# Joining the value products of a group's first and second tick into one burst

## What is computed

```python
x = x + 0.5 * ffn(layernorm(x))      # sigmoid(xr @ W_r.T) * (relu(xk @ W_k.T)**2 @ W_v.T), xr, xk mix x with the row before
q, k, v = split(layernorm(x) @ W_qkv + b_qkv)      # 16 heads, rotary positions on q and k
att = softmax(where(causal, q @ k.T / 4, -1e9))
x = x + (att @ v) @ W_proj + b_proj
x = x + 0.5 * ffn(layernorm(x))
```

## Time and profile before

| | |
|---|---|
| median of the runs | 3116.66 us (the lowest 3114.29) |
| profiled execution | 3112.07 us, span 3110.3 us |
| PE busy | 2962.3 us, 95% of the span |
| DVE busy | 2475.0 us, 80% |
| ACT busy | 2159.2 us, 69% |
| POOL busy | 1566.6 us, 50% |

### The profile page before, as it was taken

The page is one execution under the profiler, slowest core; times in us unless marked ns, Lnnn a source line. Parts: engine busy times, 40 slices in busy tenths (PEclk is TensorE's granted clock), DMA queues, the critical chain, the costliest instruction groups (busy, mean ns, idle before and its releaser), DMA issues.

```text
span 3110.3 us, 56224 instructions
## 1 busy us (share of the span) xinstructions
PE 2962.3 (95%) x18245; PEld 1665.9 (54%) x18245; DVE 2475.0 (80%) x7302; ACT 2159.2 (69%) x4802; POOL 1566.6 (50%) x2190
## 2 busy tenths in 40 slices
PE   6899999999999999999999999999999999999997
PEld 4444555555555555555555555555555555555444
DVE  3888888888888888888888887888888888887872
ACT  4477777777777777777777777777767777777664
POOL 5455555555455455555555455454555555454323
PEclk9899999999999999999999999999999999999999
DMA  3443343343434352342443333343442532433421
GB/s 99 79 84 65 64 100 66 83 90 72 86 77 88 69 97 67 76 99 60 91 87 68 88 77 84 80 85 76 79 93 59 98 81 67 93 76 71 83 60 39
DMA packets 202585, 245.49 MB, mean 79 GB/s; under 512 B 68405, under 2 KB 104245, under 8 KB 202293
## 3 DMA queue, kind: packets, MB, share of 16 engines
q1 hardware_dynamic: 202293, 241.90, 37.5%
HBM read 53.48 MB, written 51.38 MB: 34 GB/s over the span
## 4 chain that ended last, share of the span: by engine, by line
PE 66%; DVE 12%; ACT 8%; POOL 6%; issue 6%; DMA 1%; SPq 1%; POOLq 0%; DVEq 0%; ACTq 0%
PE ps_y L735 14%; PE ps_s L704 12%; PE ps_m L714 11%; PE ps_d L794 7%; PE ps_d L788 6%; PE ps_d L791 5%; PE ps_d L800 5%; ACT pt_sb L830 4%; DVE ps_m L943 3%; PE ps_d L781 3%; PE ps_d L742 2%; DVE mx_sb L946 2%; PE ps_d L804 2%; POOL pt_sb L1075 2%; DVE dif_sb L974 2%
## 5 line engine op out<-in xcount | busy, mean ns | idle before, releaser
L830 ACT ACTIVATE pt_sb<-ps_s 128x512 f32<-128x512 f32 (+1 forms) x3039 | 1451.6, 495 | 816.9 <-PE ps_s L704 806.7
L943 DVE CUSTOM_DVE_ANT_0 ps_m<-ps_m,mask_sb 128x128 f32<-128x128 f32 (+3 forms) x2048 | 990.3, 498 | 370.7 <-PE ps_m L714 355.9
L704 PE MATMUL ps_s<-qr_sb,kr_sb 99*128 99x512 bf16 (+1 forms) x3039 | 994.5, 329 | 50.4 <-ACT pt_sb L830 39.3
L714 PE MATMUL ps_m<-kr_sb,qr_sb 96*128 96x512 bf16 (+3 forms) x3072 | 1000.1, 329 | 37.9 <-DVE mx_sb L943 27.7
L946 DVE TENSOR_REDUCE mx_sb<-ps_m 128x1 f32<-128x512 f32 x1024 | 697.9, 682 | 105.7 <-PE ps_m L714 97.3
L1075 POOL TENSOR_SCALAR_AFFINE_SELECT pt_sb<-pt_sb 128x512 f32<-128x512 f32 x512 | 331.4, 647 | 833.8 <-ACT pt_sb L830 833.3
L735 PE MATMUL ps_y<-pt_sb,v_sb 128*32 128x512 f32 (+3 forms) x6144 | 589.9, 494 | 3.6 <-POOL pt_sb L1075 2.7
L704 PEld LDWEIGHTS ps_s<-qr_sb,kr_sb 99*128 99x128 bf16 x3039 | 291.8, 96 | 510.0 <-issue 229.7
L714 PEld LDWEIGHTS ps_m<-kr_sb,qr_sb 96*128 96x128 bf16 x3072 | 302.0, 98 | 319.2 <-DVE mx_sb L943 71.1
L800 PE MATMUL ps_d<-axn_sb,wqk_sb 128*128 128x256 f32 x1024 | 305.3, 396 | 3.9 <-ACT axn_sb L872 3.9
L735 PEld LDWEIGHTS ps_y<-pt_sb,v_sb 128*32 128x32 f32 x6144 | 154.6, 109 | 285.9 <-issue 258.3
(11 more groups left out here) (96 smaller groups left out, 3465.5 us busy)
## 6 DMA issues: line engine op xcount, KB each, us to landing
kr_sb<-part_sb SPq DMA_DIRECT2D x378, 128.0 KB, 4.4
qr_sb<-part_sb SPq DMA_DIRECT2D x378, 128.0 KB, 4.7
y_way<-yt_sb SPq DMA_DIRECT2D x128, 256.0 KB, 2.7
sw_sb<-qb_sb SPq DMA_DIRECT2D x496, 64.0 KB, 2.0
x_sb<-x SPq DMA_DIRECT2D x64, 256.0 KB, 2.8
yn_sb<-y_way SPq DMA_DIRECT2D x64, 256.0 KB
den_sb<-r_way SPq DMA_DIRECT2D x64, 256.0 KB
out<-x_sb SPq DMA_DIRECT2D x64, 256.0 KB, 2.2
```

The source lines that it names most:

```text
L704: eng.matmul(score_bank(slot)[:, 0:width], kr_sb[0:KR + NP, n % RS, j, kb * P:(kb + 1) * P], qr_sb[0:KR + NP, n % RS, j, q0:q0 + width], s ...
L714: eng.matmul(ps_m[:, u % NM, 0:width], qr_sb[0:KR, n % RS, j, i * P:(i + 1) * P], kr_sb[0:KR, n % RS, j, piece * QC:piece * QC + width], s ...
L830: eng.activation(pt_sb[:, buffer, j, column:column + width], score_bank(slot)[:, 0:width], ACT.Exp, scale=SCALE).then_inc(exped, 1)
L943: eng.tensor_tensor_reduce(ps_m[:, u % NM, 0:width], ps_m[:, u % NM, 0:width], mask_sb[:, m0:m0 + width], 1.0, -3e38, ALU.add, ALU.max, be ...
```

## The change

Tick 0 is put into the burst of tick 1. The burst that stood in slot 7 goes; the one in slot 11 has 16 instructions in place of 8, first those of tick 0, then those of tick 1, and raises `pved` by two. The planner does not read `BURSTS`, so the order of everything else stays as it is, on every engine. It holds for all 64 groups.

```diff
-BURSTS = [(0,), (1,), (2, 3), (4, 5), (6, 7), (8, 9), (10, 11)]
+BURSTS = [(0, 1), (2, 3), (4, 5), (6, 7), (8, 9), (10, 11)]
```

## The result

| | before | after |
|---|---|---|
| median | 3114.29 us (3110.61 to 3116.66) | 3164.51 us (3162.86 to 3166.68) |
| profiled execution, span | 3110.3 us | 3161.3 us |
| ratio | | 1.0163, 95% interval 1.0148 to 1.0178 |

The joined burst makes the kernel 1.6% slower, some 50 us by the medians and 51.0 us from span to span. The forecast was 3157, with 3120 to 3174 as the range. Direction and mechanism came as forecast; the loss was put at 40 us and is 50.

A forecast was written before the change was run, and what follows sets the result against it. PE, 95% busy, was taken as the bound, held in places by DVE and ACT. 33.9 (39 groups) + 2.0 (three) + 3.8 (first groups) + 0 (others) = 39.7 us on 3116.66: 3156.4, say 3157; range 3120 to 3174.

The forecast's parts named there:

- The cost of the joined burst: Slot 11: the longer burst takes 1.65 us, priced from ticks 8 and 9, against 0.78 for tick 1: 0.87 more.
- The advance of 0 in the 39 groups: Slots 10 and 11: DVE's maxima hold PE, so PE gains no time by slot 11; 0.87 each, 33.9 us.
- DVE gapless, so the maximum comes at the same time: Slots 7 to 11: DVE works off earlier work without gaps, so PE, free 1.09 us earlier, meets the same maximum.
- The advance in the first groups: A batch's first group, slot 9: xt_sb from ACT limits PE's gain to 0.58 of 1.09; cost 0.29, 13 groups, 3.8 us.
- The nine other groups, the start and the end: Nine groups at the kernel's start and end, -0.22 to +0.87 each: 0 together, bounds -2.0 and +7.8.
- Nothing is paid back after slot 11: Slots 12 on: PE's later waits shift with PE, so none of the 0.87 us comes back; taken as 0.
- the 42 groups: Groups held by DVE in slots 10 and 11: 39 at 0.87 (33.9 us), three with 0.2 us slack at 0.67 (2.0).
- The likeliest case: Whole kernel: the forecast itself, 3143 to 3170 us, chance 0.52.
- the third rival: All groups: no advance, 55.7 us, plus tenths in slots 12 to 19 from starved DVE and ACT; 3172 to 3190, chance 0.18.
- 0.22 us for each extra burst: Each group: one change of PE's tiling mode in and out, 0.12 exit and 0.10 entry, saved if all 1.09 is usable.

The follow-up runs named there:

- the addition alone: Kernel before with tick 0's value products made a second time at the head of slot 11's burst, slot 7's burst kept: 3166.78 us, ratio 1.0167.
- The reliefs: Two-burst and joined kernels, DVE's maxima of slots 3-8 over 128 columns: 3115.15, 3135.7 us; also POOL's cosine product over an eighth: 3116.86, 3118.84.
- join_third: Kernel before with the joined burst in slot 8 in the third group of each batch alone (16 groups): 3112.73 us, ratio 1.0000.
- join_third_late: Kernel before with the joined burst in slot 8 only in the third groups of batch elements 2 to 13 (12 groups): 3111.82 us, ratio 0.9984.
- relief_split: Kernel before, two bursts kept, with DVE's maxima of the units in slots 3 to 8 taken over 128 columns only: 3115.15 us, ratio 1.0007.
- the removal alone: Kernel before with slot 7's burst left out in groups 1 to 63 and nothing added: 3115.03 us, ratio 0.9995.

## Why the prediction was right, and where it was off

**The cost of the joined burst** was put at 0.87 and is 0.86 in every kind of group (the addition alone). The pair of ticks 8 and 9 was a true price for it.

**The advance of 0 in the 39 groups.** Held: 0.86 us lost in the regular ones, 36.1 in all against 33.9, some 5 of it the clock's (below). The step "DVE gapless, so the maximum comes at the same time" was the right test; the two timelines above show it to 0.01 us. The reliefs show it as a cause for the third group, and for the fourth only both together. For the second it is read from the waits alone; in the kernel after, PE stands there for exps too, 0.25 us in slot 9 on average.

I had called DVE's stretch of work DVE's own. Its length was partly POOL's, in the kernel before already. DVE and POOL in the fourth group of the earlier trace rows:

```profile
1571.91 1.15 DVE L974 SCALAR_TENSOR_TENSOR dif_sb<-dif_sb,mur_sb,fxn_sb 128x256 f32<-128x256 f32 x1
1572.98 0.68 DVE L997 TENSOR_TENSOR sw_sb<-sw_sb,sin_sb 128x512 f32<-128x512 f32 x1
```

```profile
1571.34 1.44 POOL L1116 TENSOR_TENSOR qb_sb<-qb_sb,cos_sb 128x512 f32<-128x512 f32 x1
```

The product of L974, 0.48 us in the median, takes 1.15 and ends 0.28 us after the cosine product (1573.06 against 1572.78). The sine product comes behind both and takes its 0.68; only in the relieved kernels is it the one that is held. In the third group of the earlier trace rows the sine product of 1.14 us ends at 1524.87, 0.53 us after POOL's select of tick 0:

```profile
1523.70 0.64 POOL L1075 TENSOR_SCALAR_AFFINE_SELECT pt_sb<-pt_sb 128x512 f32<-128x512 f32 x1 [1.25 <-ACT pt_sb L830]
```

That did not change the forecast, since all this was under way before the burst: the same rows in the kernel after are 1.15 and 1.14 us long.

**The advance in the first groups** was mis-sized: 0.58 forecast, 0.40 measured (0.86 - 0.46), 13 x 0.17 = 2.2 us. I let PE start when its input was written. It starts 0.14 us later, and here the wait is new, so the delay counts. The last 0.04 us are not explained.

**The nine other groups, the start and the end** were put at 0, with +7.8 as the bound; they took 3.3 + 1.0 + 2.2 = 6.5 us. Most of it is group 0 with 5.2, and that is the clock, not the burst. Before, group 0 has PE busy for 65.47 of 78.60 us at a mean granted clock of 0.93; after, for 71.15 of 83.80 us at 0.86, with the same 348 instructions. The start differs by that much between kernels that are the same there: group 0 is 4.1 us longer than before in the profile of `join_third` (clock 0.88) and 0.5 shorter in that of `join_third_late` (0.93).

**Nothing is paid back after slot 11.** Held: slots 12 to 47 differ by 0.00 in the regular groups, and the addition alone costs 51.8 of 55.7. This was the step that I was least sure of.

**What was missing** in the sum, beside the 0.17 of the first groups, is the clock: three second groups (17, 29 and 53) took 2.4 to 2.6 us where the others took 0.86, some 5 us together. With 2.2 of the first groups, 6.5 of the edges and 2.6 in the 42 groups (36.1 + 2.4 against 33.9 + 2.0, these three counted), the sum of 39.7 becomes 51.0. Three second groups and group 0 make some 10 of the 11.3 us that the sum was short; other groups of the edges go both ways. So a part of the miss is what the clock happened to be in one profile. The likeliest case's own range, 3143 to 3170, held; the third rival, dearer by starved dense steps, did not come: DVE stood 1.24 us as it foresaw, but no later wait grew from it.

## What to carry to other kernels

An engine that is busy for 95% can still be held in a stretch of a few slots, and there its work costs no time, up to the end of what the other engine has in hand: look at the stretch between the place a piece of work leaves and the place it goes to, and ask if the engine that hands over there has gaps. If it has none, the leaving work gains nothing and the arriving work costs all. Work that seems to be cut up at a price (0.22 us for each extra burst) may be the cover that lets another engine catch up, so price its removal and its addition apart, by two small experiments. Taking away what holds the engine may only uncover the next one that is level with it, as ACT's exps in the second groups. And judge such a move group by group: one and the same edit gave -0.59 us in one kind of group and +1.35 in another.

## What the runs showed of the hardware

**DVE and POOL on SBUF.** DVE's sine product (float32, two inputs in SBUF), when it starts while POOL's cosine product is running, ends 0.55 us after it: 1.76 us with 1.21 of overlap, 0.80 with 0.26 when the cosine product is cut to an eighth, 0.69 alone. The tail is the same for both overlaps, so the sine product makes next to no progress meanwhile, and its length in a profile is not its own. The rows above show the same with POOL's select (0.53 us after it) and with the product of L974, half as wide (0.28). Who starts first matters: in `relief_split` at 191.38 the sine product starts 0.05 us ahead of the cosine product and takes its 0.69, and the cosine product takes 1.77 where it took 1.44. The Trainium skill (SBUF — State Buffer, Who interferes with whom) has the shared ports as an exclusive lock, also for a DVE instruction with both inputs in SBUF against a POOL instruction that reads it; the trace agrees.

**The clock, with short waits before it.** In the kernel after, three stretches at the lower of the two levels (1.2 GHz) stand in second groups, where PE has no dense work in slots 8 to 11. The view by windows around one of them (us, then busy time of PE, PEld, DVE, ACT, POOL, the granted clock, DMA):

```profile
925.00:929.50 4.50, 4.50 (x37) 2.78 (x36) 3.37 (x8) 4.04 (x9) 1.53 (x3) 1.00 0.34 97
929.50:933.00 3.50, 2.53 (x14) 1.31 (x12) 3.47 (x12) 2.80 (x9) 3.14 (x4) 1.00 0.90 172
933.00:936.40 3.40, 3.04 (x17) 0.70 (x17) 1.70 (x7) 0.75 (x2) 2.63 (x4) 0.54 0.85 149
```

PE was busy without a break until 929.5, then 2.53 of 3.50 us, with waits of 0.25 and 0.53 and the first part of one of 0.55; in the next 3.4 us the clock is 0.54 of full speed. The joined burst falls into it:

```profile
933.90 3.05 PE L735 MATMUL ps_y<-pt_sb,v_sb 128*32 128x512 f32 x16
```

3.05 us in place of 1.71. In the removal alone, with still less work in those slots, seven second groups were hit. So PE work that is free by the waits is not always free by the clock, which I had not counted. That the waits make the clock fall is not shown, and what makes it fall in one second group and not in the next was not tried.
